# A two-layer adaLN + MoE kernel: expert slots padded to 64 instead of 128, with mixed tiles of two experts

## The reference

```
layer 0: cond: x @ (sum_g cond[b,g] * W[g] * mask).T + bias, per batch b
         ffn:  8 linear experts (256 -> 256), top-2 of softmax(router), plus a bias from probs
layer 1: cond: x @ W_base.T + b_base + 2 * sum_e cond[b,e] * (x @ A_e.T) @ B_e.T
         ffn:  sum of 2 shared experts for all tokens
               + top-2 of 8 routed experts, weights normalised over the two
               expert(h) = (silu(h @ Wg) * (h @ Wu)) @ Wd,   F = 352
```

## Time and profile before

| | us |
|---|---|
| median of 3 runs | 379.49 (378.72 to 379.71) |
| the profiled execution | 378.77 |
| its span in the trace | 377.0 |
| TensorE busy in it | 357.7 (95%) |
| DVE / ACT / POOL busy | 238.8 / 166.1 / 154.2 |
| granted TensorE clock, mean | 0.994 |

### The profile page before, as it was taken

How to read it: one execution, slowest core, us unless ns; L and a number is a source line. 1 busy time by engine, 2 the same in 40 slices (tenths; PEclk the granted TensorE clock), 3 DMA queues, 4 the chain that set the end, 5 groups by cost and what they waited for, 6 DMA issues and landing times.

```text
span 377.0 us, 7974 instructions
## 1 busy us (share of the span) xinstructions
PE 357.7 (95%) x2713; PEld 225.4 (60%) x2714; DVE 238.8 (63%) x594; ACT 166.1 (44%) x286; POOL 154.2 (41%) x241
## 2 busy tenths in 40 slices
PE   7998999999999999989999999999999999999992
PEld 3543544455454454555447677777777777776561
DVE  1357999676766646778775455565555565546476
ACT  1045376567555765543442333333333333323560
POOL 3000564665647532000020365565665555532642
PEclk9999999999999999999999999999999999999997
DMA  7985113433443420100000122222222222212942
GB/s 217 377 330 203 54 53 119 150 92 122 141 151 128 136 69 0 58 0 2 0 28 2 44 86 84 70 84 78 75 83 80 73 78 78 80 42 74 353 161 111
DMA packets 18038, 39.26 MB, mean 104 GB/s; under 512 B 2976, under 2 KB 9376, under 8 KB 17888
## 3 DMA queue, kind: packets, MB, share of 16 engines
q1 hardware_dynamic: 13552, 28.71, 22.8%
q0 software_dynamic: 3744, 10.23, 8.7%
q10 hardware_dynamic: 720, 0.02, 0.1%
HBM read 29.65 MB, written 9.31 MB: 103 GB/s over the span
## 4 chain that ended last, share of the span: by engine, by line
PE 72%; DVE 16%; DMA 4%; ACT 3%; issue 3%; SPq 0%; DVEq 0%
PE bank L1000 58%; PE bank L1147 4%; PE bank L1245 3%; DVE prod L904 2%; PE bank L1016 2%; PE bank L1229 2%; ACT acts L582 2%; DVE x L892 2%; DMA w1s<-results 2%; DVE x L777 2%; DVE acts L910 1%; DMA x<-wc 1%; PE bank L1076 1%; DMA results<-yb,row_out 1%; ACT sil L572 1%
## 5 line engine op out<-in xcount | busy, mean ns | idle before, releaser
L442 POOL TENSOR_TENSOR w1s<-piece,w1s 128x170 f16<-128x170 f32 x128 | 61.6, 521 | 78.2 <-ACT piece L532 78.2
L1000 PE MATMUL bank<-w0s,hs 128*128 128x512 f16 x384 | 86.0, 379 | 1.2 <-DVE x L777 1.2
L1000 PE MATMUL bank<-w1s,rT 128*128 x468 | 76.2, 313 | 1.6 <-DVE rT L964 1.6
L451 POOL DMA_INDIRECT rows<-token_store,row_in x39 | 37.9, 971 | 86.1 <-DVE row_in L874 47.5
L777 DVE SCALAR_TENSOR_TENSOR x<-bank,coef,x 128x256 f32<-128x256 f32 x128 | 54.8, 478 | 19.4 <-PE bank L1000 19.1
L1000 PEld LDWEIGHTS bank<-w0s,hs 128*128 128x128 f16 x384 | 36.9, 98 | 43.8 <-DVE x L777 1.9
L1000 PE MATMUL bank<-hs,w1s 128*128 128x512 f16 x264 | 59.6, 379 | 2.1 <-DVE prod L904 2.1
L1000 PEld LDWEIGHTS bank<-w1s,rT 128*128 128x128 f16 x468 | 44.0, 98 | 22.1 <-issue 2.1
L456 POOL DMA_INDIRECT results<-yb,row_out x39 | 38.5, 987 | 37.1 <-ACT yb L606 37.1
L1000 PE MATMUL bank<-w1s,aT 128*128 (+1 forms) x351 | 44.8, 273 | 0.8 <-DVE aT L957 0.8
L600 ACT ACTIVATE ract<-prod 128x352 f16<-128x352 f32 x39 | 19.4, 497 | 58.5 <-DVE prod L970 33.6
(11 more groups left out here) (149 smaller groups left out, 405.5 us busy)
## 6 DMA issues: line engine op xcount, KB each, us to landing
piece<-w SPq DMA_DIRECT2D x16, 680.0 KB, 3.9
w1s<-results SPq DMA_DIRECT2D x6, 512.0 KB, 8.3
x<-wc SPq DMA_DIRECT2D x4, 512.0 KB, 7.0
w1s<-xT SPq DMA_DIRECT2D x4, 512.0 KB, 11.0
w1s<-w SPq DMA_DIRECT2D x4, 512.0 KB, 10.1
token_store<-xrow SPq DMA_DIRECT2D x4, 512.0 KB, 3.3
out<-x SPq DMA_DIRECT2D x8, 256.0 KB, 2.2
x<-x SPq DMA_DIRECT2D x1, 1536.0 KB, 11.7
```

What stands on the lines that cost most here:

```text
L442: ins = nc.gpsimd.tensor_tensor(w1s[:, LO, at], piece[:, i % 2, part], w1s[:, HI, at], ALU.subtract)
L451: pool.indirect_dma_start(rows[:, i % 2], None, token_store, bass.IndirectOffsetOnAxis(row_in[:, i:i + 1], 0)).then_inc(s_row[i % 2], 16)
L1000: mm = nc.tensor.matmul(out_ap, l, r, start=(i == 0), stop=(i == len(terms) - 1))
```

## The change

The padding of each expert's slots is to 64 instead of 128. TILES becomes ((4096 + 8 x 63) // 64 + 1) // 2 = 36. An expert's slots are counted in halves of 64: `whole` is its number of full tiles, and what is over is at most one odd half. First in slot order stand all whole tiles, by expert, then the odd halves, by expert. FULL = 28 tiles have surely one expert; the last MIXED = 8 may have two, one in each half. They are not run last: every fourth tile (`CYCLE` = 4; `mixed(i)`: 4, 8, ..., 32) is a mixed one, and `slot_tile(i)` and `owner(i)` say which slots and which entry of `te` it has.

A mixed tile's upper half takes its weights from `w1s` as before. Its lower half takes them from a static buffer over `xrow` (`own_gu`, `own_dn`), to which SP copies them from `w1s` by two DMAs a mixed tile (704 KB and 384 KB). On PE each matmul of a mixed tile becomes two with 64 weight columns, to PSUM partitions 0-63 and 64-127 (`pair`).

The loop has TURNS = 7 turns of four steps, with seven register loads from `te7`.

The slot chain: `groups` scans 16 entries in four steps, for whole tiles and odd halves; `jumps` makes the distance that a token beyond its expert's whole tiles jumps; `slots`, `hot_tiles`, one eighth of `hot_lanes` and `tile_experts` are cut up and put between `prod(i)` and `acts` LO of items 5 to 15. PE's `down(0)` waits for `jumps(1)` and not for `slots`; `inverse()` and `slot_tokens` come after item 13; PE's first loads of `te` come after `gate_up(17)`. The rows of tiles 0 and 1 are transposed in `down(1)` ahead of its last quarter, into banks 0 and 2, and copied in `accumulate(1)` (`first_rows`). `side(i)` is i % 2.

```diff
-    TILES = (N * K_TOP + E * (P - 1)) // P
+    HALF = P // 2
+    TILES = ((N * K_TOP + E * (HALF - 1)) // HALF + 1) // 2
+    FULL = (N * K_TOP // HALF - E) // 2
+    OWNERS = FULL + 2 * (TILES - FULL)
+    MIXED = TILES - FULL
+    CYCLE = TILES // (MIXED + 1)
+    TURNS = MIXED - 1
...
+            for n in range(MIXED):
+                at = nc.values_load_multi_w_load_instructions(te[0:1, FULL + 2 * n + 1:FULL + 2 * n + 2], ...
+                if n:
+                    sp.wait_ge(sm["s_ru"], CYCLE * n + 1)
+                sp.dma_start(own_gu, w1s[:, :, bass.ds(at, KT * 2 * F)]).then_inc(sm["s_own_gu"], 16)
+                if n:
+                    sp.wait_ge(sm["s_rd"], CYCLE * n + 1)
+                sp.dma_start(own_dn, w1s[:, :, bass.ds(at + KT * 2 * F, FT * D)]).then_inc(sm["s_own_dn"], 16)
...
+            def jumps(step):
+                rank = bank[6][:, 0:NT * E].rearrange("p (t e) -> p t e", t=NT)
+                if step == 0:
+                    ...
+                if step == 1:
+                    nc.vector.scalar_tensor_tensor(t2[:], per_expert(base[:, 0]), float(HALF), rank, ALU.mult, ALU.add)
+                    link(nc.vector.tensor_tensor(t1[:], rank, per_expert(room[:]), ALU.is_ge))
+                    link(nc.vector.tensor_tensor(t1[:], t1[:], per_expert(jump[:]), ALU.mult))
+                    nc.vector.tensor_tensor(t2[:], t2[:], t1[:], ALU.add).then_inc(sm["s_ranked"], 1)
...
+            between = {5: lambda: jumps(0), 6: lambda: slots(0), 7: lambda: hot_tiles(0, 0), 8: lambda: hot_lanes(7),
+                       9: lambda: hot_tiles(0, 1), 10: lambda: hot_tiles(1), 11: lambda: hot_tiles(2, 0),
+                       12: lambda: hot_tiles(2, 1), 13: lambda: tile_experts(0), 14: lambda: tile_experts(1),
+                       15: lambda: tile_experts(2)}
...
+            def pair(outs, upper, lower, s):
+                for i in range(len(upper)):
+                    for out_ap, terms in zip(outs, (upper, lower)):
+                        l, r = terms[i]
+                        mm = nc.tensor.matmul(out_ap, l, r, start=(i == 0), stop=(i == len(terms) - 1))
+                mm.then_inc(sm[s], 1)
...
+                        if c == 1 and q == TPB - 1:
+                            first_rows(0)
+                            first_rows(1)
...
+                            pair((bank[2 * par + g][0:HALF, 0:F], bank[2 * par + g][HALF:P, 0:F]),
+                                 [(rT[:, par, a, k, 0:HALF], w1s[:, b, bass.ds(gate_at + (k * 2 + g) * F, F)])
+                                  for k in range(KT) for a, b in PASSES],
+                                 [(rT[:, par, a, k, HALF:P], own_gu[:, b, (k * 2 + g) * F:(k * 2 + g + 1) * F])
+                                  for k in range(KT) for a, b in PASSES], done)
...
+            with pe.Fori(0, TURNS) as j:
+                d0, d1, d3, g1, g2, d2, g3 = experts(te7[0:1, bass.ds(j, 1), :].rearrange("p a b -> p (a b)"))
+                step(j * CYCLE + 3, 1, d0, d3)
+                step(j * CYCLE + 4, 0, d1, g1)
+                step(j * CYCLE + 5, 1, d2, g2, down_own=j * 16 + 16)
+                step(j * CYCLE + 6, 0, d3, g3, gate_own=j * 16 + 32)
```

More of the change, by code:

```diff
@@ L256, in build_program @@
             "s_acc",
+            "s_own_gu",
+            "s_own_dn",
             "s_ra",
@@ L325, in again, with mixed, slot_tile, owner @@
             return not isinstance(i, int) or i >= 2
+        def mixed(i):
+            return i % CYCLE == 0 and 0 < i < TILES
+        def slot_tile(i):
+            return FULL + i // CYCLE - 1 if mixed(i) else i - i // CYCLE
+        def owner(i):
+            return FULL + 2 * (i // CYCLE - 1) if mixed(i) else slot_tile(i)
         def landed(i, par):
@@ L386, in _ @@
             keep(3)
+            sp.wait_ge(sm["s_idx"], 1)
+            sp.wait_ge(sm["s_tok"], 16 * B)
+            sp.wait_ge(sm["s_pclo"], NP)
+            for n in range(MIXED):
+                at = nc.values_load_multi_w_load_instructions(
+                    te[0:1, FULL + 2 * n + 1:FULL + 2 * n + 2], engines=(nc.sync.engine,), min_val=SHARED * WE,
+                    max_val=(NEXP - 1) * WE,
+                    skip_runtime_bounds_check_because="the table's entries are clamped where it is made")[1][0]
+                if n:
[4 more added lines that the diff above has]
+                sp.dma_start(own_dn, w1s[:, :, bass.ds(at + KT * 2 * F, FT * D)]).then_inc(sm["s_own_dn"], 16)
             sp.wait_ge(s_put[0], 16 * ((TILES + 1) // 2))
@@ L844, in hot_lanes, with hot_tiles @@
             def hot_lanes(k):
                 dve.wait_ge(sm["s_pclo"], NP)
-                for n in range(k * ENTRIES // TPB, (k + 1) * ENTRIES // TPB):
+                for n in range(k * ENTRIES // 8, (k + 1) * ENTRIES // 8):
                     nc.vector.tensor_scalar(hot_lo[:, n], lane16[:], slot_lo[:, n:n + 1], None, ALU.is_equal)
-            def hot_tiles(step):
-                shape = [P, ENTRIES, TILES]
+            def hot_tiles(step, part=0):
+                n = slice(part * NT, (part + 1) * NT)
+                shape = [P, NT, TILES]
@@ L907, in shared_dve @@
                     h_lo(1, B - 1)
+                if between is not None:
+                    between()
                 dve.wait_ge(sm["s_ahi"], i + 1)
@@ L937, in _ @@
                 if i == 5:
[L938 to L941, removed]
+                    jumps(1)
+                if i == 6:
+                    slots(1)
+                if i == 13:
                     slot_tokens()
-                if i == 14:
-                    tile_experts()
                 if i in DOWN:
@@ L1257, in _ @@
             pe.wait_ge(sm["s_acc"], TPB + 1)
             for s in range(-2, 3):
[L1259 to L1264, removed]
-            for s in range(3 + 2 * LOOPS, TILES + 1):
-                step(s, s % 2, places[s - 1 - (TILES - 3)], None)
+                step(s, s % 2, places[owner(s - 1)] if s >= 1 else None, places[-1 if mixed(s + 2) else owner(s + 2)],
+                     gate_own=16 if mixed(s + 2) else None)
@@ L1267, in _ @@
+            for s in range(3 + CYCLE * TURNS, TILES + 1):
+                step(s, s % 2, low[0] if mixed(s - 1) else places[owner(s - 1) - last.start],
+                     places[owner(s + 2) - last.start] if known(s + 2) else None,
+                     down_own=16 * MIXED if mixed(s - 1) else None)
                 if s == TILES - 2:
```

202 lines of the change are left out of this document (130 added, 72 removed).

## The result

The changed kernel takes 375.28 us (median of 4 runs, 374.84 to 375.49) against 379.4 for the kernel before: the ratio is 0.9895, interval 0.9865 to 0.9926, so 4.1 us or 1.1% faster. Forecast were 371.4, 8 us faster. The sign was right and half of the gain was missing: 375.28 lies outside the forecast's own range of 368 to 374.5, where rivals D and E were expected. All times here are medians of executions at full speed; one execution of e5_onecopy, 520.81 us at a granted clock of 0.66, is left out.

What follows compares the result with a forecast made beforehand. TensorE, busy 357.7 of 377.0 us, was taken as the bound. Terms -10.0 + 6.3 - 4.2 + 0.2 = -7.7 us gave 371.1 from 378.77, stated as 371.4 for the median; own range 368 to 374.5.

Steps and rivals of the forecast that it cites:

- D: New wait: the DVE walk gives nothing, or loop turns starve TensorE of instructions by 0.5 us; 375.5; 0.13 with E.
- E: Mixed tiles: copies or rows come late, 0.5 us for each tile; 375.4 us; chance 0.13 together with D.
- Part 1: Loop of routed tiles: three tiles fewer at 3.33 us of TensorE each, -10.0 us.
- Part 2: Matmuls of eight mixed tiles: a pair of 64-column matmuls costs one wide matmul, 0; bounds 0 to 22.2 us.
- B: Mixed tiles' matmul pairs: the halves don't overlap in fp16, price 22.2 us; 393.6 us; chance 0.06.
- C: Mixed tiles' weight loads: each pair's second load is exposed, 0.106 us, 17.8 in all; 389 us; chance 0.06.
- Part 3: Mixed tiles: TensorE empties between narrow and wide work, 32 changes at 0.2 us, +6.3 us; bounds 0 to 9.6.
- Parts 4 and 5: Shared part and entry to the routed tiles: rearranged slot chain and earlier first rows remove TensorE waits, -4.2 us; bounds 0 and -5.4.
- Part 5: First two row tiles: transposes moved into `down(1)`, so 1.6 us of `rT` waits and issue gaps go.
- Part 6: Copies and registers in the loop: copies 0; seven register loads a turn covered by TensorE's queue, +0.2 us, bounds 0 to 6.3.
- The copies: Eight 704 KB and eight 384 KB SBUF copies on SP's queue: done before they are needed, 0 us.
- The end: After the last tile: the order of puts landing, reload of `results` and combine is not touched.

Runs made afterwards that it cites:

- e5_onecopy: e2 with the weight copies made for the first mixed tile only, the other seven reusing those weights: 369.3 us, ratio 0.9744.
- e4: e2 with the mixed tiles' products made at full width with the upper half's expert alone: 365.37 us, ratio 0.9628.
- e6: e2 with all upper-half matmuls of each group ahead of the lower-half ones, instead of by turns: 376.62 us, ratio 0.9929.
- e2: The changed kernel with te7 rows of eight words, loaded as two fours, the second after the turn's second step: 369.96 us, ratio 0.9765.
- e7: e2 with the first two row tiles transposed and copied where the kernel before does it: 370.46 us, ratio 0.9752.
- e1: The changed kernel with te7 rows padded from 7 to 8 words, all 8 loaded at the start of a turn: 369.54 us, ratio 0.9744.
- e8: e2 with 24 small matmuls of 8 columns added at the start, to shift TensorE's program fetches: 368.93 us, ratio 0.9723.
- e10: The changed kernel unaltered, run once more in the same rounds as e7: 375.74 us, ratio 0.989.

## Why the prediction was right and wrong

**Part 1**, three tiles: right. The wide steps are still 3.33 us.

**Part 2**, pairs for the price of one: right, by the trace after and by e4 and e6. The rivals B and C would have shown 3.6 or 2.9 us for 24 matmuls; there are 1.91. The rule of the Trainium skill that was weighed there ("TensorE: Matmul & The Clock Gate", Part 3) does not hold for the halves of the columns: in e2 the two loads for a pair, 0.11 us each, both start at 229.31, while the pair of the same moment runs for 0.31.

**Part 3**, changes of width: the right mechanism, mis-sized, 6.3 us for 3.6 (32 x 0.2 is 6.4, a slip of 0.1). The one place in the trace before gave 0.2; that it had fp32 operands and four narrow matmuls ahead of it may be why, but no run shows it. In the trace after, the distance from the last matmul before a change to the first behind it is 0.245 us for 0.149 out of gate/up and 0.204 for 0.109 out of `down`, 0.1 more, with a few hundredths in the matmuls behind it. This error was in the forecast's disfavour, by 2.7 us.

**Parts 4 and 5**, slot chain and first rows: right, -4.4 for -4.2, counted from the same item. `down(1)` started at 196.32 for 196.1, gate/up of tile 0 at 204.19 for 203.99, and the wait that stayed was the 0.26 named. Part 5 alone is 1.5 us by e7, for 1.6.

**Part 6**, registers: this is the step that failed. It was priced at 0.2 us, with a bound of 6.3, and it is 5.9. The reason given was that steps with a turn between them took 3.33 us like the others, "so TensorE's queue covers it". That was right and told only that a load of 0.33 us is covered. The bound held by luck: its 0.9 us was the longest wait in 200 to 345, and in 220 to 330, the loop, there was none at all. What the edit changed was the load itself, four words on a multiple of 16 bytes to seven words mostly off it, and I priced the count of turns and not the duration of one load. The trace before had the number: its load behind the loop, three words, took 0.78 us, more than twice that of four, which already says that words don't cost alike.

```profile
L1195 PEldq TENSOR_LOAD <-te x1: 777/777/777, 333.4 to 333.4; - x1
```

Rival D had the place but gave the matmuls of a turn as its reason; e1 changes no matmul and removes the wait. D's time (375.5) is near by luck: it had 0.5 us a turn for 0.9, and kept the 6.3 of part 3.

The Trainium skill bears on this too: "Runtime: NRT & Kernel Launch", the section "Instruction fetch mechanics", puts a register load at some 0.2 us a register, for the registers loaded at launch from HBM, where here they come from SBUF. The trace comes near it for words off the boundary (1.7/7 = 0.24 us) and not for four aligned ones (0.33 for all four).

**The copies**, also of part 6: right, nothing (e5). Once they may have come near it: in e1 a gather of rows issued at 217.84, 0.5 us behind a copy, is what TensorE waited for at 224.15, and that step lost 0.3 us. No other trace has a wait for rows or copies in the loop.

**The end** was called untouched, and it took 1.0 us more in the profiled execution. The second reload DMA, after and before:

```profile
341.06 1.51 SPq L435
```
```profile
346.05 0.51 SPq L394
```

Queue 8 has 16 packets for 14, the program of TensorE having become longer, and one of its fetches fell on the moment in which SP issues the reload. None of my rivals had this. That the issue is long when a fetch starts just behind the first DMA is shown by twelve traces and by moving the fetch in e8; how one holds up the other is not settled. Nor is this all of the end: the last reload DMA of the chain took 8.06 us to land for 7.00 and the last put 2.41 for 2.95, and e10, with an issue of 1.29 us, has no longer an end than the kernel before. The same page of the Trainium skill says that the sequencer fetches its program by its own DMA queue in blocks of 16 KB; the trace agrees (queue 8, 16 packets, 0.26 MB).

With 5.9 in place of 0.2, 3.6 in place of 6.3, -4.4 in place of -4.2, +0.4 ahead of the shared part and +1.0 for the end the sum is -3.5, the measured difference of the spans. The wide range 365 to 378 held, because the 2.7 us too many in part 3 made up for half of part 6; the own range 368 to 374.5 and the turn of 14.1 did not.

## What to carry to other kernels

Price a load of registers in a loop by its words and by the address of the first one, and pad its table's rows to a multiple of 16 bytes: here that one word was worth 5.7 us, more than the whole change had brought. A resource that shows no wait has only shown that its present load is covered; when an edit makes that load longer, its price starts where the cover ends, so read the cover's length (here between 0.6 and 1.0 us), not its absence from the waits. Halves of the array's columns can take two experts' work at the price of one, if the program alternates between them.

## What the runs showed of the hardware

- Register loads on TensorE's sequencer: 1 word 0.31 us; 4 words on a multiple of 16 bytes 0.33, off it 1.00 to 1.02; 8 on it 0.59 to 0.60; 7 on it 1.06 to 1.08, off it 1.70 to 1.92; 5 off it 1.24. These fit one read of 0.25 to 0.3 us for each four words if the first is on a multiple of 16 bytes, and for each single word otherwise. The first load of each kernel, from the start of `te`, is 0.2 us longer than that (4 words 0.52 to 0.53, 5 words 0.79 to 0.80); why is open.
- What a turn's step then takes longer, by the load's length: nothing at 0.33, at most 0.05 us at 0.6, 0.1 to 0.3 at 1.0 to 1.08, 1.0 to 1.4 at 1.7 to 1.9.
- Matmuls of the free half of the columns start ahead of up to three queued ones of the other half (e6). A change between 128 and 64 columns costs 0.11 us.
- A block of TensorE's program fetched just as SP issues a DMA goes with an issue of 1.15 to 1.51 us in place of 0.51.
